# Reordering the setup, the remainders of w1 and w2 and some later waits of a fused attention, routing and expert kernel on one core

## The reference

```python
def attention(x, Wq, bq, Wk, bk, Wv, bv, Wo, bo, sigma):
    q, k, v = x @ Wq.T + bq, x @ Wk.T + bk, x @ Wv.T + bv
    r_attn = softmax(einsum('bhwd,bhkd->bhwk', q, k) - gw * dist(w))
    c_attn = softmax(einsum('bwhd,bwgd->...', q, k) - gw * dist(h))
    return (r_attn @ v + c_attn @ v) @ Wo.T + bo
x = x + attention(layernorm(x))
t = x.reshape(2048, 256); n = layernorm(t)
gates = softmax(n @ wg); idx = argmax(gates)
# at most 256 tokens an expert, in order of position
t = t + combine(gate * (relu(dispatch(n) @ w1[e]) @ w2[e]))
```

## Time and profile before

| what | value |
| --- | --- |
| median of three runs | 187.66 us (187.43 to 188.41) |
| the profiled execution | 187.77 us |
| its span, first to last instruction | 185.8 us |
| mean granted TensorE clock | 0.997 |
| busy: PE, DVE, ACT, POOL | 95%, 77%, 61%, 66% |

### The profile page before, as it was taken

How to read it: one execution, slowest core, us unless ns; L and a number is a source line. 1 busy time by engine, 2 the same in 40 slices (tenths; PEclk the granted TensorE clock), 3 DMA queues, 4 the chain that set the end, 5 groups by cost and what they waited for, 6 DMA issues and landing times.

```text
span 185.8 us, 3936 instructions
## 1 busy us (share of the span) xinstructions
PE 175.7 (95%) x1372; PEld 168.8 (91%) x1372; DVE 142.4 (77%) x394; ACT 113.6 (61%) x275; POOL 122.5 (66%) x156
## 2 busy tenths in 40 slices
PE   7889999999999999999999979999999999999980
PEld 7788999999989988779999979999999999999970
DVE  0497758889898899763747799899699996997820
ACT  3347866968858787715568892791874935745000
POOL 4276364786888988588258599748468495369552
PEclk9999999999999999999999999999999999999998
DMA  5797996731111319393898139139184293611010
GB/s 167 232 371 247 296 238 180 298 115 60 62 59 56 116 59 314 98 336 117 250 350 290 63 93 378 38 99 377 65 267 184 69 359 133 186 47 45 4 68 28
DMA packets 23860, 31.66 MB, mean 170 GB/s; under 512 B 2728, under 2 KB 20649, under 8 KB 23840
## 3 DMA queue, kind: packets, MB, share of 16 engines
q1 hardware_dynamic: 21264, 26.32, 43.9%
q0 software_dynamic: 1616, 4.24, 6.4%
q10 hardware_dynamic: 960, 0.85, 1.3%
HBM read 23.02 MB, written 8.55 MB: 170 GB/s over the span
## 4 chain that ended last, share of the span: by engine, by line
PE 73%; DVE 11%; ACT 4%; DMA 4%; issue 3%; POOL 2%; POOLq 1%; SPq 0%; DVEq 0%; ACTq 0%
PE banks_v L634 8%; PE banks_v L635 7%; PE banks_v L641 7%; PE banks_o L706 6%; PE bank_pT L634 4%; PE bank_pT L641 4%; PE bank_pT L635 4%; DMA sl<-in_x 4%; PE bank_s L641 3%; PE bank_q L641 3%; PE bank_q L634 3%; PE bank_s L634 3%; PE bank_s L635 3%; PE bank_q L635 3%; PE bank_xT L641 2%
## 5 line engine op out<-in xcount | busy, mean ns | idle before, releaser
L984 ACT ACTIVATE w_high<-w_in_sb 128x1024 fp32r<-128x1024 f32 x22 | 22.9, 1056 | 8.0 <-DMA w_in_sb<-in_L_ffn_w 8.0
L591 POOL DMA_INDIRECT out<-y,goal x16 | 17.1, 1069 | 13.4 <-issue 7.9
L573 POOL TENSOR_TENSOR w_low<-vx,w_high 128x1024 fp32r<-128x1024 f32 x8 | 20.1, 2532 | 4.8 <-ACT w_high L984 4.7
L573 POOL TENSOR_TENSOR w_low<-w_in_sb,w_high 128x1024 fp32r<-128x1024 f32 x7 | 17.5, 2513 | 8.1 <-ACT w_high L984 8.0
L1364 DVE TENSOR_TENSOR w_low<-w_in_sb,w_high 128x1024 fp32r<-128x1024 f32 x12 | 17.0, 1415 | 5.9 <-ACT w_high L984 5.9
L506 POOL DMA_INDIRECT slots<-row,slot x14 | 14.4, 1025 | 7.0 <-DVE slot L1277 3.6
L706 PE MATMUL banks_o<-vx,pT 128*128 128x266 f32 x64 | 16.5, 397 | 0.2 <-issue 0.2
L634 PE MATMUL banks_v<-w_high,h_high 128*128 128x256 f32 x64 | 16.1, 288 | 0.0
L635 PE MATMUL banks_v<-w_high,h_low 128*128 128x256 f32 x64 | 15.7, 283 | 0.0
L634 PE MATMUL bank_pT<-w_high,h_high 128*128 128x256 f32 x56 | 14.0, 288 | 1.0 <-POOL w_low L573 1.0
L1085 ACT ACTIVATE h_high<-bank_xT 128x512 fp32r<-128x512 f32 x8 | 4.7, 594 | 15.5 <-PE bank_xT L641 15.5
(11 more groups left out here) (245 smaller groups left out, 660.2 us busy)
## 6 DMA issues: line engine op xcount, KB each, us to landing
w_in_sb<-in_L_ffn_w SPq DMA_DIRECT2D x12, 1024.0 KB, 7.0
vx<-in_L_ffn_w SPq DMA_DIRECT2D x4, 1024.0 KB, 5.6
sl<-slots SPq DMA_DIRECT2D x9, 266.0 KB, 4.8
slots<-empty SPq DMA_DIRECT2D x8, 266.0 KB, 4.3
sl<-in_x SPq DMA_DIRECT2D x8, 256.0 KB, 7.2
out<-row SPq DMA_DIRECT2D x7, 256.0 KB, 2.8
table_in<-in_tables SPq DMA_DIRECT2D x1, 292.0 KB, 6.2
w_in_sb<-in_L_conv_Wk SPq DMA_DIRECT2D x1, 256.0 KB, 3.5
```

The source lines that it names most:

```text
L573: step = nc.gpsimd.tensor_tensor(w2_low[e % 2][:, half, :], w2_raw[e % 2][:, half, :], w2_high[e % 2][:, half, :].bitcast(f32), ALU.subtract)
L591: nc.gpsimd.indirect_dma_start(out_rows, bass.IndirectOffsetOnAxis(ap=goal[j][:, c:c + 1].bitcast(u32), axis=0), y[j][:, c, :], None, boun ...
L984: nc.scalar.activation(high[e % 2][:, half, :], raw[:, half, :], ACT.Copy).then_inc(ready, 1)
```

## The change

- SP: the load of the second x goes behind bq and wg, the third behind Wv, w1[0] ahead of the fourth x; bo's row load comes from POOL's queue to SP's, with a semaphore of its own; the zero fill of the slots waits for one half of w1[0] instead of two. On ACT's queue ident goes ahead of Wo.
- PE: the 9 warming products after the fold go; Wo's transposes, qbias and wgsum stand there, and image 0's transposes behind them. After the loop, counts(5) follows the first product of attention_out(6), and counts(6) the whole of attention_out(7,0).
- ACT: `split_w1(0, [0])` goes behind image 1's high part, m is rounded ahead of the exponentials of image 0, query(1) comes ahead of `normalised_x(2)`, and `split_w1(0, [1])` is moved into turn 1, behind `normalised_x(3)`.
- DVE: the norms of the images 1 to 4 are each moved later (image 4's into turn 1); image 7's second maxima go ahead of `place(5)`; the second half of the last expert's w2 remainder comes from POOL.
- POOL: `first_rstd(3)` goes behind the first two remainders of w1[0], `first_rstd(4)` between the third and the fourth, with two more instructions; the remainders of w1[1] of turns 4 and 5 go behind the scatter, of turn 6 one before and one behind; expert 1's second half of w2 goes ahead of the first scatter of y.

The diff, with lines of its surroundings left out:

```diff
...
 X_GROUPS = tuple((2 * i, 2 * i + 2) for i in range(B))
-SETUP_GROUPS = 5
-WARM_UP, WARM_WAIT = 10, 9
+SETUP_GROUPS = 4
+WARM_UP = 10
 EARLY = B - 3
 W1_TURNS = (3, 4, 5, 6)
-W1_LOW = {4: (0,), 5: (1,), 6: (2, 3)}
 OFF = 1e30
...
             "const_in", "eye_in", "weights_in", "wv_in", "small_in", "wg_in", "token_in"))
-        bq_in, rows_in = sem("bq_in"), sem("rows_in")
+        bq_in, rows_in, bo_in = sem("bq_in"), sem("rows_in"), sem("bo_in")
         x_in = [sem(f"x_in{j}") for j in range(len(X_GROUPS))]
         w1_high_ready, w1_split, w2_high_ready, w2_split = (sem(n) for n in ("w1_high_ready", "w1_split", "w2_high_ready", "w2_split"))
-        first_w2_low = sem("first_w2_low")
+        first_w2_low, last_w2_low = sem("first_w2_low"), sem("last_w2_low")
         row_free, y_free = sem("row_free"), sem("y_free")
...
             load_x(0)
-            load_x(1)
             with nc.allow_non_contiguous_dma(reason="bias columns of 128"):
                 sp.dma_start(wg_sb[:, :, :], wg.rearrange("(c p) e -> p c e", p=P)).then_inc(wg_in, 16)
-                load_x(2)
+                load_x(1)
                 for columns, b in ((bv_sb, bv), (bo_cols, bo)):
             sp.dma_start(wv_sb, matrix(Wv)).then_inc(wv_in, 16)
+            load_x(2)
+            sp.dma_start(w1_in_sb[:, :, :], w1_view[0]).then_inc(w1_in, 16)
+            sp.dma_start(bo_sb[:, :], bo[None, :].to_broadcast([P, D])).then_inc(bo_in, 16)
             load_x(3)
-            sp.dma_start(w1_in_sb[:, :, :], w1_view[0]).then_inc(w1_in, 16)
             load_x(4)
             for g in range(5, B):
...
             sp.sem_inc(row_free, 4)
-            sp.wait_ge(w1_high_ready, DC)
+            sp.wait_ge(w1_high_ready, 1)
             sp.wait_ge(empty_ready, 1)
             for e in range(E):
...
             nc.gpsimd.dma_start(sigma_sb[:, :], sigma[None, :].to_broadcast([P, 1])).then_inc(rows_in, 16)
-            nc.gpsimd.dma_start(bo_sb[:, :], bo[None, :].to_broadcast([P, D])).then_inc(rows_in, 16)
             norm = Chain(pool, norm_step)
...
             first_rstd(2)
-            first_rstd(3)
             first_w1_low(0)
             first_w1_low(1)
-            first_rstd(4)
+            first_rstd(3)
             pre = Chain(pool, pre_step)
...
             first_w1_low(2)
+            first_rstd(4)
             pool.wait_ge(u_ready, 4)
...
             for i in range(2, B):
                 x_and_bias(i)
-                for n in W1_LOW.get(i, ()):
-                    second_w1_low(n)
+                if i == 6:
+                    second_w1_low(2)
                 if i < B - 1:
                     scatter_rows(i - 2)
+                    if i >= 4:
+                        second_w1_low((0, 1, 3)[i - 4])
                 else:
...
                     step = nc.gpsimd.tensor_tensor(w2_low[e % 2][:, half, :], w2_raw[e % 2][:, half, :], w2_high[e % 2][:, half, :].bitcast(f32), ALU.subtract)
-                if part == 1 or e == 0:
+                if part == 1 or e in (0, E - 1):
                     step.then_inc(w2_split, 1)
             def slot_rstd(e, turn):
...
             for j in range(2):
             pool.wait_ge(x2_stored_last, 16)
+            split_w2(1, [1])
             scatter_y(0)
-            split_w2(1, [1])
             slot_rstd(3, 4)
             for e in range(1, E - 1):
-                split_w2(e + 1, range(2))
+                split_w2(e + 1, range(2) if e + 1 < E - 1 else [0])
                 if e + 3 < E:
...
                     step.then_inc(pT_made, 1)
-            def attention_out(i, t, between=None):
+            def attention_out(i, t):
                 pe.wait_ge(pT_ready, 2 * i + (t + 1 if i == B - 1 else 2))
...
                 for c in range(2):
-                    if between and c:
-                        between()
                     step = nc.tensor.matmul(ps_o[:, t, 0:VW], pT[:, c, t * P:(t + 1) * P], v_sb[i % 2][:, c, 0:VW], start=c == 0, stop=c == 1)
...
             step.then_inc(fold_a, 1)
-            keep_warm(WARM_WAIT)
             pe.wait_ge(eye_in, 32)
-            transpose_x(0)
             for c in range(DC):
                 for m in range(DC):
...
             for c in range(DC):
             step.then_inc(wgsum_made, 1)
+            transpose_x(0)
             pe.wait_ge(a_ready, 1)
...
             scores(B - 1)
+            attention_out(B - 2, 0)
             counts(B - 3)
-            attention_out(B - 2, 0)
             attention_out(B - 2, 1)
             transpose_prob(B - 1, [1])
-            attention_out(B - 1, 0, between=lambda: counts(B - 2))
+            attention_out(B - 1, 0)
+            counts(B - 2)
             attention_out(B - 1, 1)
             def dispatch_5(t):
...
                 pe.wait_ge(w2_split, e + 1)
+                if last:
+                    pe.wait_ge(last_w2_low, 1)
                 if e == 0:
...
         def _(act):
             act.dma_start(wq_sb, matrix(Wq)).then_inc(weights_in, 16)
+            act.dma_start(ident_sb[:, :], eye).then_inc(eye_in, 16)
             act.dma_start(wo_sb, matrix(Wo)).then_inc(eye_in, 16)
-            act.dma_start(ident_sb[:, :], eye).then_inc(eye_in, 16)
             def normalised_x(i):
...
             nc.scalar.activation(m_high[:, :, VW:MW], wgc[:, :, 0:E], ACT.Copy).then_inc(gate_m_high_ready, 1)
+            transposed_x(1)
             split_w1(0, which=[0])
-            transposed_x(1)
-            split_w1(0, which=[1])
-            exponentials(0, [0])
             act.wait_ge(fold_m, 1)
             nc.scalar.activation(m_high[:, :, 0:VW], ps_v[:, :, 0:VW], ACT.Copy).then_inc(m_high_ready, 1)
-            exponentials(0, [1])
+            exponentials(0)
+            query(1)
             normalised_x(2)
-            query(1)
             values(0)
             for i in range(1, B - 1):
...
                     normalised_x(i + 2)
+                if i == 1:
+                    split_w1(0, which=[1])
                 if i + 1 in W1_TURNS:
...
             def spread():
-                dve.wait_ge(rows_in, 32)
+                dve.wait_ge(rows_in, 16)
                 setup.mark(nc.vector.tensor_tensor(decay[:, 0:1], sigma_sb[:, :], sigma_sb[:, :], ALU.mult))
...
             first_norm(0)
-            first_norm(1)
             dve.wait_ge(a_high_ready, 1)
             spread()
-            first_norm(2)
-            x_low(0)
+            first_norm(1)
             dve.wait_ge(qbias_made, 1)
             dve.sem_inc(wgc_ready, 1)
+            x_low(0)
             masks()
-            first_norm(3)
             query_low(0)
...
             def bias_rows():
                 setup.mark(nc.vector.tensor_copy(ow[:, :], ps_ow))
+                dve.wait_ge(bo_in, 16)
                 nc.vector.tensor_tensor(obias[:, :], ps_obias, bo_sb[:, :], ALU.add).then_inc(b_ready, 1)
             def maxima(i, t):
...
                     place(i - 2, slot_of(i - 2)).then_inc(slot_ready, 1)
-                if 2 <= i < 5:
+                if i < 5:
                     first_norm(i + 3)
...
             maxima(0, 1)
+            first_norm(2)
             dve.wait_ge(m_high_ready, 1)
             low_part(m_low[:, :, 0:VW], ps_v[:, :, 0:VW], m_high[:, :, 0:VW]).then_inc(m_ready, 1)
-            first_norm(4)
+            first_norm(3)
             weights_both(0)
...
             maxima(B - 1, 0)
+            maxima(B - 1, 1)
             place(B - 3, place_of[2]).then_inc(placed_5, 1)
-            maxima(B - 1, 1)
             weights(B - 1, 0)
...
                     gathered_low(e + 2)
+                else:
+                    dve.wait_ge(w2_high_ready, 2 * E)
+                    half = slice(FC // 2, FC)
+                    nc.vector.tensor_tensor(w2_low[1][:, half, :], w2_raw[1][:, half, :], w2_high[1][:, half, :].bitcast(f32),
+                                            ALU.subtract).then_inc(last_w2_low, 1)
                 output_rows(e, 1 if e == 1 else e + 1)
```

## The result

| | before | after |
| --- | --- | --- |
| median | 187.55 us (4 runs, 187.37 to 188.41) | 192.92 us (4 runs, 192.37 to 194.9) |
| ratio | | 1.0291, interval 1.025 to 1.0331 |
| the profiled execution, its span | 187.77, 185.8 | 192.87, 191.0 |
| mean granted clock of that execution | 0.997 | 0.984 |

The change makes the kernel slower by 5.4 us. The forecast was 189.2, with a range up to 191.0: the direction was right, the size and the range were not.

What follows compares the result with a forecast made beforehand. TensorE, busy 95% of the span, was taken as the bound. Sum: 187.77 - 0.4 (setup) + 2.7 (load) + 0.5 (turns) - 1.1 (expert 1) - 0.3 (last expert) = 189.17, so 189.2 us; range 186.8 to 191.0.

Steps and rivals of the forecast that it cites:

- The turn of the load: Turn 3: w1[0]'s second half, split in turn 1, delays w1[1]'s load, so TensorE idles before query(4); +2.7 us.
- rival C: Turns 2 and 3: w1[1] lands sooner or its wait has more cover; 188.2 us in all, chance 0.13.
- Setup: Up to scores(1): image 0's remainder comes earlier, a gain mostly given back; -0.4 us, bounds 0 and -1.2.
- it gives most of the gain back: Setup: GpSimd's first two w1 remainders, now around 19 to 22, eat most of up to 1.2 us by scores(1).
- Rival E: Setup: the second x or Wo comes late and the 0.4 gain goes; 189.6 us in all, chance 0.10.
- The turns' holds: Turns 4 to 6: w1[1]'s remainders behind the scatters hold ranked instead of slot, and image 5's choice; +0.5 us.
- Rival B: Setup and turns 4 to 6: short vector instructions come ahead of GpSimd's moved subtractions; 187.0 us in all, chance 0.22.
- Expert 0: Its second product starts right behind GpSimd's chain of one-hots, six scatters and a remainder, without slack; no term of its own.
- Expert 1: Second half of w2 subtracted ahead of the first scatter of y, so TensorE's 0.98 wait goes; -1.1 us.
- the scatter behind it sends rows out for which nobody waits: Expert 1: putting the first scatter of y behind the w2 subtraction was taken to delay nobody; no cost in the sum.
- The last expert: Half of its w2 remainder goes to the vector engine, so TensorE's wait before the product goes; -0.3 us.
- rival D: Setup: TensorE's clock falls to 1.2 GHz around the thin products and query(0), 1.8 us more; 191.0 us, chance 0.07.

Runs made afterwards that it cites:

- mending that one place: Changed kernel with GpSimd's first two remainders of w1[0] ahead of the norm of image 2: 191.45 us, ratio 1.0226.
- the order that keeps the clock: Changed kernel with 9 warming products, then image 0's transposes, ahead of the thin products, and image 0's remainder early on the vector engine: 191.68 us, ratio 1.021.
- the fill: Changed kernel with one fill of a dead tile on the vector engine ahead of its two pieces of w2[0]'s remainder: 192.98 us, ratio 1.029.
- the mended whole: Changed kernel with w1's second half, SP's wait, GpSimd's first remainders, the turns, the dispatch and TensorE's setup order taken back or mended: 185.61 us, ratio 0.9885.

## Why the prediction was wrong

- **The turn of the load, right.** +2.64 for +2.7, by the path given: SP's issue, the landing, the activation engine's wait, query(4). The landing took 5.24, so rival C is out. With it goes the estimate of 4.4 from the Trainium skill's page "DMA: Bandwidth & Descriptors", section "Anatomy of one DMA — SWDGE (gpsimd) path", a fit for transfers that GpSimd issues. Taking that half back removes all of the 2.64. What the term lacks is the clock: in one trace it fell behind this wait, and the turns cost another 1.7.
- **Setup, wrong in sign (-0.4, measured +0.38).** The step that failed is "it gives most of the gain back": the hold was seen, its place too, and I let it eat a gain at most. The two held instructions took 0.87 and 1.05 for 0.17 each, and TensorE lost more than the gain by it, as mending that one place shows (-1.05). Rival E, that nothing is gained, had the price nearer.
- **The turns' holds, right in kind, mis-sized (+0.5, measured +1.22).** ranked was held by 0.69, 1.54 and 1.00 where I put 0.8; I credited slot's relief as a whole against it, though slot releases a scatter and ranked stands ahead of the low part that query(i+1) needs. Rival B, which has the holds go, is refuted by 56.13, 63.59 and 71.99. The rule of the Trainium skill's page "SBUF — State Buffer", section "SBUF: two separate sides", has the instruction that began first hold the other; 56.13 and 71.99 agree, but in the row of 63.59 the one that was held began 0.41 first by the trace's start times.
- **Expert 0, not in the sum (measured +1.16).** The prediction names the place as one without slack, and priced only what comes ahead of the scatters, not the scatters. The trace of the kernel before shows two held scatters, of 1.84 (119.34) and 1.17, but among the later ones of y, behind which TensorE never waits; the prediction did not take them up. The box on DMAs issued by GpSimd in the section "SBUF: two separate sides" of the same page of the Trainium skill has their descriptors wait while the vector engine has the port; the rows of 2.03 and 1.63 against 0.97 agree, though the box speaks of operations in a two-port mode, such as copies, and these are subtractions.
- **Expert 1, right (-1.35 for -1.1), and its cost behind it missed (+1.42).** The step that failed is "the scatter behind it sends rows out for which nobody waits". SP waits for them, two experts' loads are queued behind that wait, and the kernel's text says so (L430). I looked for who waits on TensorE's side and not on the load queue.
- **The last expert, -0.31 for -0.3, cause not shown.** The trace of the kernel before without its nine products keeps both halves on GpSimd and is 0.36 shorter in this stretch all the same, with no wait before the last expert's second product. So the number may be luck.
- **The clock, rival D, given 0.07.** It fell in the changed kernel's profile, at the place named, and was given too little. Its price of 1.8 was too high for that execution, though two deeper falls cost 1.4 to 1.8 at image 3's transposes, against the six traces with a full clock: with the order that keeps the clock, 0.50 of it shows at image 1's transposes and 0.12 at image 3's, inside setup's +0.38. It is not why the forecast missed in this trace.

The range's upper end was that of one rival. That several terms end high together, and that the change makes waits which the sum has no term for, was left out of it; the two that it has no term for make 2.6 of the 3.8 that were missing.

What stays open: why the scatter behind the fill was held though it began 0.17 ahead of the subtractions, why a vector instruction that began ahead of GpSimd's subtraction was held by it, and why the clock falls in some executions of one and the same program.

## What to carry to other kernels

A piece of work moved ahead of a transfer delays that transfer, and the queue that waits for its landing is a reader too: list the waits of the loading queue, not only those of the engines that compute. When a GpSimd subtraction is moved, look up which short vector instruction it will lie beside and what stands behind that one; the hold is the same everywhere, and what it costs is set by the place. A reordering that comes out slower can hold parts that pay: split by the starts of one engine's milestones, this one had -1.05 in setup and -1.35 at expert 1 in it, and the mended whole is 1.1% faster than before.

## What the runs showed of the hardware that I had not expected

- A GpSimd scatter that begins while one of the vector engine's subtractions of weights is under way ends 0.84 to 0.88 behind it (48 of 48 in the kept traces, up to 2.03 instead of 0.97); one that began ahead took 0.97 to 1.08 (76 of 77; the other 1.63, with a fill running).
- Holds repeat within one pair of instructions: two ranked beside two remainders took 2.40 for 0.36, and one subtraction of 128x512, begun 0.53 ahead of GpSimd's, 3.52 for 0.68.
- TensorE's granted clock fell behind the thin products in setup, while the kernel before keeps it full in that window; nine warming products ahead of them did not prevent it (5 of 8 executions had a mean clock of 0.974 or 0.975), and with those products and image 0's transposes ahead of the thin ones it was full (5 of 5). In one trace it fell in the loop, behind 1.75 of idle.
